# A macaron transformer layer on eight cores: a third gate-weight buffer, a bf16 gate tile, and one exponential instruction for four key tiles instead of two

## The reference

```python
def _L0_ffn_ref(x, wq_gate, s_gate, wq_up, s_up, wq_down, s_down):
    gate = silu(_qlinear(x, wq_gate, s_gate))     # (w - 128) * scale, 2048 -> 5632
    up = _qlinear(x, wq_up, s_up)
    return _qlinear(gate * up, wq_down, s_down)   # 5632 -> 2048
...
x = x + 0.5 * _L0_ffn_ref(_layernorm(x), ...)
x = x + _L0_attn_ref(_layernorm(x), ...)          # 16 heads of 128, causal softmax, + residual
x = x + 0.5 * _L0_ffn_ref(_layernorm(x), ...)
```

## Time and profile before

| what | value |
|---|---|
| median of 5 runs | 7337.54 us (7193.67 to 7607.9) |
| the profiled execution | 6741.95 us; span of its slowest core 6740.4 us |
| spans of the 8 cores | 6714.3 to 6740.4 us |
| mean granted TensorE clock | 0.913 to 0.916 of full |
| busy, share of the span | TensorE 83%, VectorE 21%, ScalarE 14%, GpSimd 5% |
| DMA | 757.76 MB per core, mean 112 GB/s |

### The profile page before, as it was taken

One profiled execution on the slowest core, in us unless ns is written; L12 is line 12 of the kernel. 1 busy time (PEld: TensorE's weight loads), 2 busy tenths in 40 slices (PEclk: granted clock), 3 DMA queues, 4 the chain that ended last, 5 costly groups with the idle time before them and its releaser, 6 DMA issues.

```text
span 6740.4 us, 99038 instructions; the slowest of 8 cores (6714.3 to 6740.4 us)
## 1 busy us (share of the span) xinstructions
PE 5613.9 (83%) x27920; PEld 2676.0 (40%) x27920; DVE 1426.9 (21%) x2645; ACT 932.0 (14%) x1728; POOL 367.1 (5%) x695
## 2 busy tenths in 40 slices
PE   5888898988976766776776778688699999899999
PEld 2333343433332323433433553355344444344444
DVE  3111112100000033433442332332400000200000
ACT  0000000000000012221332433144100000000000
POOL 1111101000000020010010000000000000000000
PEclk8999999999988877778888989898899999899999
DMA  6677688555555442434433343521422244122233
GB/s 111 130 133 133 136 179 174 126 127 127 132 141 139 121 101 83 133 88 140 129 67 98 106 133 87 148 67 60 115 76 79 76 133 134 65 79 76 77 127 113
DMA packets 368748, 757.76 MB, mean 112 GB/s; under 512 B 42064, under 2 KB 111184, under 8 KB 362064
## 3 DMA queue, kind: packets, MB, share of 16 engines
q1 hardware_dynamic: 188496, 461.94, 22.6%
q0 software_dynamic: 99072, 136.36, 15.5%
q10 hardware_dynamic: 80640, 153.13, 6.2%
HBM read 734.49 MB, written 153.09 MB: 132 GB/s over the span
## 4 chain that ended last, share of the span: by engine, by line
PE 61%; DMA 25%; issue 5%; DVE 5%; ACT 2%; POOL 0%; SPq 0%; DVEq 0%; ACTq 0%; POOLq 0%
PE f_pp L537 14%; PE f_pp L482 13%; PE f_pp L491 13%; DMA a_wA<-wq_sc 4%; PE a_pA L763 3%; PE a_pB L789 3%; DMA a_wB<-wo_sc 3%; DMA f_cvt<-wo_t 3%; DMA f_cvt<-wv_t 2%; DMA f_cvt<-wq_t 2%; PE a_pL L1061 2%; DMA f_cvt<-wk_t 2%; PE a_pPV L1054 2%; PE a_pB L893 2%; PE a_pA L954 2%
## 5 line engine op out<-in xcount | busy, mean ns | idle before, releaser
L482 PE MATMUL f_pp<-f_rbf,f_wg 128*128 128x512 bf16 x5632 | 1295.8, 388 | 211.2 <-DVE f_wg L448 115.8
L537 PE MATMUL f_pp<-f_g,f_wd 128*128 128x512 bf16 x5632 | 1249.9, 385 | 142.9 <-DMA f_wd<-wd_sc 110.9
L491 PE MATMUL f_pp<-f_rbf,f_wu 128*128 128x512 bf16 x5632 | 1247.6, 380 | 0.0
L482 PEld LDWEIGHTS f_pp<-f_rbf,f_wg 128*128 128x128 bf16 x5632 | 548.8, 99 | 942.9 <-issue 322.5
L537 PEld LDWEIGHTS f_pp<-f_g,f_wd 128*128 128x128 bf16 x5632 | 556.5, 99 | 835.8 <-issue 194.2
L491 PEld LDWEIGHTS f_pp<-f_rbf,f_wu 128*128 128x128 bf16 x5632 | 552.0, 98 | 668.0 <-issue 6.0
L500 DVE SCALAR_TENSOR_TENSOR f_g<-f_pp,s_su,f_gt 128x1024 bf16<-128x1024 f32 x176 | 226.0, 1284 | 2350.1 <-PE f_pp L491 1752.3
L497 ACT ACTIVATE f_gt<-f_pp,s_sg 128x1024 f32<-128x1024 f32 x176 | 196.0, 1113 | 2398.5 <-PE f_pp L482 1206.4
L893 PE MATMUL a_pB<-a_ao,a_wB 128*128 128x256 bf16 x2048 | 275.4, 291 | 123.0 <-DMA a_wB<-wo_sc 121.2
L543 DVE SCALAR_TENSOR_TENSOR f_rc<-f_pp,s_sde,f_rc 128x1024 f32<-128x1024 f32 x64 | 82.2, 1284 | 1268.6 <-PE f_pp L537 986.2
L954 PE MATMUL a_pA<-a_xk,a_wA 128*128 128x256 bf16 x2048 | 251.9, 277 | 78.9 <-DMA a_wA<-wq_sc 77.4
(11 more groups left out here) (131 smaller groups left out, 2888.5 us busy)
## 6 DMA issues: line engine op xcount, KB each, us to landing
f_wg<-wg_sc SPq DMA_DIRECT2D x132, 512.0 KB, 3.4
f_wu<-wu_sc SPq DMA_DIRECT2D x132, 512.0 KB, 3.4
f_wd<-wd_sc SPq DMA_DIRECT2D x48, 1408.0 KB, 7.5
a_wA<-wq_sc SPq DMA_DIRECT2D x256, 256.0 KB, 3.7
a_wB<-wo_sc SPq DMA_DIRECT2D x256, 256.0 KB, 4.6
a_wA<-wk_sc SPq DMA_DIRECT2D x128, 256.0 KB, 3.0
a_wB<-wv_sc SPq DMA_DIRECT2D x128, 256.0 KB, 2.7
f_wg<-wg_t POOLq DMA_DIRECT2D x88, 256.0 KB, 5.4
```

The lines of the kernel that those rows point to most:

```text
L482: e.matmul(ppg[:, o:o + w], gw[:, dc * 128:(dc + 1) * 128], F.rbf[dc][:, o:o + w], start=(dc == 0), stop=(dc == NDC - 1)),
L491: e.matmul(ppu[:, o:o + w], uw[:, dc * 128:(dc + 1) * 128], F.rbf[dc][:, o:o + w], start=(dc == 0), stop=(dc == NDC - 1)),
L537: e.matmul(ppd[:, o:o + w], dw[:, hc * 128:(hc + 1) * 128], F.g[hc][:, o:o + w], start=(hc == 0), stop=(hc == NHC - 1)),
```

## The change

1. `f_gt`, the silu tile, becomes bf16 instead of f32 (ScalarE writes it, VectorE reads it), in both FFNs.
2. `f_wg` gets three buffers instead of two, used in turn (`parg = hc % 3`); `f_wu`, `f_wd` and the PSUM tiles still alternate between two. Per partition `f_gt` gives back 4 KB (two tiles of 2 KB less each) and the third `f_wg` takes 4 KB.
3. In `front`, one exponential takes the whole batch (up to 1024 columns, two banks) instead of one for each two key tiles.

```diff
-    F.gt = [sb(f"f{u}_gt{i}", [128, TtF], F32) for i in range(2)]
+    F.gt = [sb(f"f{u}_gt{i}", [128, TtF], BF16) for i in range(2)]
-    F.wg = [sb(f"f{u}_wg{i}", [128, NDC * 128], BF16) for i in range(2)]
+    F.wg = [sb(f"f{u}_wg{i}", [128, NDC * 128], BF16) for i in range(3)]
...
             par = hc % 2
-            gw, uw = F.wg[par], F.wu[par]
+            parg = hc % 3
+            gw, uw = F.wg[parg], F.wu[par]
...
-                        writes=[f"fwg{par}h{hx}"], tag="cvG")
+                        writes=[f"fwg{parg}h{hx}"], tag="cvG")
...
-                    reads=[f"wg:{hc}"], writes=[f"fwg{par}h0", f"fwg{par}h1"])
+                    reads=[f"wg:{hc}"], writes=[f"fwg{parg}h0", f"fwg{parg}h1"])
...
-                for sb0 in range(0, tbw, 2):
-                    sw = min(2, tbw - sb0)
-                    P.add("act", lambda e, tb0=tb0, sb0=sb0, sw=sw, pten=pten,
-                          PT=PT, ub=ub: e.activation(
-                        PT[:, (tb0 + sb0) * QG:(tb0 + sb0 + sw) * QG],
-                        pten[:, sb0 * QG:(sb0 + sw) * QG],
-                        AF.Exp, scale=INV_SQRT_HD, bias=ub[:, 0:1]),
-                        reads=pbanks(pname, sb0 * QG, sw * QG) + [ubik],
-                        writes=[f"{ptk}:{tb0 + sb0 + i}" for i in range(sw)])
+                P.add("act", lambda e, tb0=tb0, tbw=tbw, pten=pten, PT=PT,
+                      ub=ub: e.activation(
+                    PT[:, tb0 * QG:(tb0 + tbw) * QG], pten[:, 0:tbw * QG],
+                    AF.Exp, scale=INV_SQRT_HD, bias=ub[:, 0:1]),
+                    reads=pbanks(pname, 0, tbw * QG) + [ubik],
+                    writes=[f"{ptk}:{tb0 + i}" for i in range(tbw)])
```

More of the change, by code:

```diff
@@ L446, in emit_ffn @@
                         c.wg_t[hc * 128:(hc + 1) * 128, o:o + hcols]),
-                        writes=[f"fwg{par}h{hx}"], tag="cvG")
+                        writes=[f"fwg{parg}h{hx}"], tag="cvG")
                     P.add("dve", lambda e, b=gw, o=hx * hcols: e.tensor_scalar(
                         b[:, o:o + hcols], b[:, o:o + hcols], -128.0, None, ALU.add),
-                        reads=[f"fwg{par}h{hx}"], writes=[f"fwg{par}h{hx}"])
+                        reads=[f"fwg{parg}h{hx}"], writes=[f"fwg{parg}h{hx}"])
                     P.dma("act", lambda e, hc=hc, b=gw, o=hx * hcols: e.dma_start(
@@ L453, in emit_ffn @@
                         b[:, o:o + hcols]),
-                        reads=[f"fwg{par}h{hx}"], writes=[f"wg:{hc}"])
+                        reads=[f"fwg{parg}h{hx}"], writes=[f"wg:{hc}"])
                 for hx in range(2):
@@ L485, in emit_ffn @@
                         start=(dc == 0), stop=(dc == NDC - 1)),
-                        reads=[f"fwg{par}h{hx}", f"frbf{dc}"], writes=pbanks(gk, o, w))
+                        reads=[f"fwg{parg}h{hx}", f"frbf{dc}"], writes=pbanks(gk, o, w))
             for dc in range(NDC):
```

## The result

The changed kernel took 7146.43 us (median of 6 runs, 6850.07 to 7635.77), against 7222.48 us of the kernel before (10 runs, those measured beside it included). It gives a ratio of 1.016 (95% interval 1.012 to 1.021): slower by 1.6%. Forecast were +0.5% and "within 2%". The sign is right, the forecast size a third of what came.

What follows compares the result with a forecast made beforehand. TensorE, busy 83% of the span, was taken as the bound, so only its waits count. Terms 0 + 2 + 21 + 9 = +32 us gave about 6774 us profiled, 7370 us as median; range 7190 to 7570 us, within 2% at 80%.

Steps and rivals of the forecast that it cites:

- Part 1 at 0: FFN: bf16 silu tile leaves VectorE's 1284 ns scalar_tensor_tensor unchanged; 0, at best -38 us.
- Part 2, gain 0: FFN gate loads: TensorE waits for VectorE's subtraction, not gate weights, so the third buffer gains 0.
- Its price, +2 us at the starts of the tiles: Three token tile starts: an extra 512 KB gate load may delay the activations; +2 us, between 0 and +12.
- Part 3, the waits: Head loops nt = 10 to 16: products with V start 0.64, 0.28, 0.47, 0.12 us later per head; 21 us.
- Part 3, the clock: Head loops nt = 10 to 16: longer fronts lower TensorE's clock only at nt = 14; +9 us.
- the term at nt = 14: Head loop nt = 14: 24% of its time at 1.2 GHz instead of 8%; +9 us.
- the fronts at nt = 10 and 12 stay shorter than the 3.22 us of nt = 14 now: 0: Head loops nt = 10 and 12: fronts of 2.7 and 2.9 us keep the clock; cost 0.
- the clock rival: Four head loops: merged waits of about 0.9 us per head bring 1.2 GHz; +180 us, 7530 us; 10%.
- ScalarE as the pace of the loops: Head loops: ScalarE sets the pace, so fewer exponentials save 41 us, 7293 us on the median's scale; 12%.
- The third buffer as a gain in runs that the trace did not show: Steady FFN steps: timed runs wait for gate weights, earlier loads return 147 us, 2%, giving 7190 us; 8%.
- The signs of being wrong: Shorter nt = 10 head; scalar_tensor_tensor under 1.1 us; nt = 10 and 12 clock below 0.9; FFN stages changing over 15 us.
- The sum: Whole kernel: 0 + 2 + 21 + 9 = +32 us, 6741.95 to about 6774 us, +0.5%; forecast 70%.

Runs made afterwards that it cites:

- C: Kernel before with bf16 silu tile and third gate buffer only outside the converting pass; converting pass 714.6 us, second token tile 704.4 us.
- E: Changed kernel, previous head's products with V moved between second and third score batch (nt = 10 to 16); loops 65.0, 74.6, 83.7, 93.1 us.
- F: Kernel before, previous head's products with V moved between second and third score batch (nt = 10 to 16); loops 65.0, 74.3, 83.7, 93.1 us.
- B: Kernel before with bf16 silu tile and three gate buffers, exponentials still in halves; ratio 1.005 (1.001 to 1.010).
- L: Changed kernel, products with V between score batches, converting pass's next loads and subtraction ahead of the scalar_tensor_tensor; undisturbed cores' median span 6536.2 us.
- M: Kernel before, products with V between score batches, converting pass's next loads and subtraction ahead of the scalar_tensor_tensor; undisturbed cores' median span 6542.0 us.
- J: Changed kernel profiled a second time, nothing altered; converting pass 737.8 us, second token tile 698.2 us, attention 2460.5 us.
- H: Kernel before profiled a second time, nothing altered; converting pass 713.9 us, second token tile 703.2 us, attention 2416.4 us.
- A: Kernel before with only one exponential per batch; ratio 1.010 (0.996 to 1.024), attention 2473.1 us, converting pass 715.5 us.
- D: Kernel before with bf16 silu tile and third gate buffer only in the converting pass; converting pass 736.6 us, second token tile 696.2 us.
- G: Kernel before with a one-element VectorE copy ahead of each gate subtraction of the converting pass; converting pass 760.7 us.

## Why the prediction was right and where it was not

**Part 1 at 0**: right. 1284 ns before and after, and in C, which has it, neither FFN stage is longer than before.

**Part 2, gain 0**: right, TensorE never waited for a gate weight. **Its price, +2 us at the starts of the tiles**: the step that failed. I asked what the extra load collides with at the start of a tile and not what the earlier issue collides with in each step. The order showed it: the gate load's two issues now stand directly behind the up load's, and in the earlier trace rows VectorE's subtraction is the one thing on TensorE's path at that moment. It cost 18 to 24 us: about 20 longer waits of 0.12 us are 2 to 3 us, and 8 to 18 gate runs of 8.75 instead of 7.07 us, 1.7 us each, are the rest.

**Part 3, the waits**: right nearly to the digit. The products were to start 2.70 us after the scores at nt = 10; a head was to take 4.65 + 0.64 = 5.29 us and takes 5.29. At nt = 12, 14 and 16 the heads at full clock take 5.94, 7.17 and 7.82 us (before 5.66, 6.67, 7.69): +0.28, +0.50 and +0.13 against the +0.28, +0.47 and +0.12 of the working. The waits add up to 68 us (42.0 and 26.1 on the two tiles) where I had 63; before they were 32.

**Part 3, the clock**: the term at nt = 14 was right (+9 us forecast; 15.3 less 7 us of waiting is 8). The step "the fronts at nt = 10 and 12 stay shorter than the 3.22 us of nt = 14 now: 0" failed: they cost 14 and 11 us (23.5 less 9.6, 15.3 less 4.2). I had compared the lengths of the fronts. What changed there is the single wait: 0.27 us before, 0.92 us after. A long wait in one piece brought the clock down although the front around it was shorter than one that had kept it. At nt = 16 it cost 2 us, so the clock came to about 35 us over the four loops where the sum had 9. This is the mechanism of the clock rival (one wait of 0.9 us per head instead of several short ones), to which I gave 10%; its full price did not come, since the loops' clock stopped at 0.85 to 0.90 and not below 0.63.

**The rivals**: ScalarE as the pace of the loops falls by the result itself, since ScalarE's busy time fell and the loops grew, and by E against F. The third buffer as a gain in runs that the trace did not show falls by B, which is slower; L against M shows no gain either.

**The signs of being wrong**: two of the four that the prediction named came. The clock of the loops at nt = 10 and 12 dropped below 0.9 (0.86 and 0.88), and an FFN stage changed by more than 15 us (+18 in the converting pass). That the time still stayed within 2% is luck as far as these two go: neither was in the sum.

**The sum**: +32 us forecast, of which 21 + 9 in attention and 2 elsewhere. Reproducible are about +44 to +58 us in attention and +18 to +24 us in the converting pass. In the second profiles (J against H) that is +62 us, 0.9%; in the first +93 us, with the second tile's 18 us. The undisturbed cores of J's timed runs have a median span of 6781.0 us against 6700.9, +80 us or 1.2%, and the ratio of the result is 1.2 to 2.1%. The two shown causes explain 62 to 82 us of that; the rest may be the second token tile or the spread between executions, and no run tells them apart.

The median itself, 7146.43 us, lies below the 7190 to 7570 us that the prediction gave it. That interval rested on five executions of the kernel before, none under 7193.67 us, while the six of the changed kernel reach down to 6850.07. Where a median of so few falls was decided by the spread between executions and not by the change; the ratio carried over to the median scale was no forecast of it.

## What to carry to other kernels

Fewer and larger instructions on an engine that is not the bound are not free: the larger one starts later and ends later, and whoever waits for its first part waits longer. Give the waiting engine other work at that place first; in E and F the size of the piece then no longer mattered.

A buffer more moves issues as well as data. Before adding one, look at what stands on the critical path at the moment when the earlier issue will now happen, and on which engines.

A wait of TensorE is to be priced with the clock behind it. Here 0.05 us of waiting per step cost twenty times as much in clock.

## What the runs showed of the hardware

GpSimd's issue of a DMA slows VectorE down beside it: two subtractions of 128x1024 bf16 took 0.85 instead of 0.75 us when GpSimd's issues ran at the same time, and those issues took 1.23 us for two instead of 0.53 each. Where VectorE had begun first (400.13), its subtraction kept its 0.75 us, and that step lost nothing. The Trainium skill's "SBUF — State Buffer" (section "Who interferes with whom") has a port pair that the two engines share as an exclusive lock; in the two steps shown, the order of who begins first agrees with it. By that lock the later one would wait for the whole of the other's instruction: the 0.10 us that VectorE lost is less than the 0.27 us that were left of the first issue, and in 61 further steps of that profile GpSimd's issue had begun just before VectorE (0.5 us of it were left) and VectorE still took 0.76 to 0.78 us. So the trace shows neither the full block nor that the order of the starts decides by itself, and the measurement decides.

A few hundredths of a microsecond of TensorE's waiting separate the steps that keep 2.4 GHz from those that lose it. Between gate runs TensorE does 14 us of matmuls and then waits. In the converting passes of before, A, C, D, E, H, J and the changed kernel, eight cores each, 1737 steps waited 1.94 or 1.95 us, and not one gate run behind them began at 1.2 GHz. In G, where nearly every wait is 1.99 us, 199 of 301 did. In the first profile of the changed kernel 174 of 344 steps waited 2.05 to 2.07 us; 66 of the gate runs behind them began at 1.2 GHz. In 173 of those 174 steps VectorE's two subtractions took 0.85 us or more and GpSimd's issue was running when they began, which is the chain from the moved load to the clock, step by step. The kernel before has 8 such steps too, one per core, and 4 of the gate runs behind them began at 1.2 GHz. The longer wait does not make the loss more frequent: 38% at 2.05 to 2.07 us in half of the steps, 66% at 1.99 us in all of them. So the wait alone does not decide each case.

The head loops say the same. One wait of 0.92 us per 5.3 us was followed by 1.2 GHz in the later half of the loop at nt = 10, where the waits of 0.27 us had not been; the first heads of that same loop, with the same wait, stayed at 2.4 GHz. What else decides was not tried.
